# A decoder layer on one core: where TensorE's waits for banks, data and copied row maxima stand

## What is computed

```python
# x: (64, 128, 128), ctx: (64, 77, 128); 16 heads of 8 features
h = layernorm(x)
q, k = rope(h @ Wq.T + bq) * 8 ** -0.5, rope(h @ Wk.T + bk); v = h @ Wv.T + bv
x = x + softmax(causal(q @ k.T)) @ v @ Wo.T + bo                 # self attention
h = layernorm(x)
x = x + softmax(q2(h) @ k2(ctx).T * 8 ** -0.5) @ v2(ctx) @ Wo2 + bo2   # cross attention, 77 keys
h = layernorm(x)
top1, e = max(softmax(h @ router_w))                             # 8 experts, the eighth adds nothing
x = x + 2 * top1 * expert_e(h) + shared(h)                       # gated, 512 hidden
```

## Time and profile before

| what | value |
|---|---|
| time, median of 3 runs | 1080.29 (1079.55 to 1080.8) |
| profiled execution | 1076.56, span 1074.7, granted clock 0.995 |
| TensorE matmul busy | 987.1 (92%) |
| VectorE / ScalarE / GpSimd busy | 870.5 / 738.3 / 631.6 |
| masks L999, matmuls | x2048, 53.1 busy, 20.5 idle before, 14.8 of it for the DMA arena<-arena |
| DMAs arena<-arena (L391) | x512, 4.0 KB each |

### The profile page before, as it was taken

One profiled execution on the slowest core, in us unless ns is written; L12 is line 12 of the kernel. 1 busy time (PEld: TensorE's weight loads), 2 busy tenths in 40 slices (PEclk: granted clock), 3 DMA queues, 4 the chain that ended last, 5 costly groups with the idle time before them and its releaser, 6 DMA issues.

```text
span 1074.7 us, 45099 instructions
## 1 busy us (share of the span) xinstructions
PE 987.1 (92%) x16200; PEld 819.5 (76%) x16201; DVE 870.5 (81%) x2853; ACT 738.3 (69%) x1557; POOL 631.6 (59%) x1488
## 2 busy tenths in 40 slices
PE   1578999999999999999999999999999889999995
PEld 1356777777777777777777777777777889999995
DVE  3367999989999999989999999999996557777774
ACT  0266887888888787888878888887875245555552
POOL 0345667776767767676677767677664224444443
PEclk9999999999999999999999999999999999999998
DMA  5222111000010000000000000100010122222220
GB/s 132 70 71 71 33 29 32 28 28 27 25 32 26 30 25 28 29 25 30 25 29 28 25 30 25 31 26 30 26 28 24 60 66 71 72 68 71 67 67 5
DMA packets 66648, 44.27 MB, mean 41 GB/s; under 512 B 24135, under 2 KB 61451, under 8 KB 66592
## 3 DMA queue, kind: packets, MB, share of 16 engines
q1 hardware_dynamic: 55424, 30.35, 10.5%
q0 software_dynamic: 5312, 12.18, 3.3%
q10 hardware_dynamic: 5856, 0.99, 0.5%
HBM read 23.96 MB, written 18.29 MB: 39 GB/s over the span
## 4 chain that ended last, share of the span: by engine, by line
PE 62%; SPq 16%; DMA 6%; DVE 6%; issue 5%; ACT 2%; ACTq 1%; POOL 1%; DVEq 0%; POOLq 0%
SPq L391 12%; PE pv L1120 9%; PE scores L1300 6%; PE scores L1305 6%; PE ro L1316 6%; DMA arena<-arena 5%; PE scores L999 5%; PE ro L1175 4%; PE scores L1161 3%; PE ro L1137 3%; PE st L1230 3%; DVE arena L641 3%; PE scores L1167 2%; PE ro L1148 2%; PE pj L1143 2%
## 5 line engine op out<-in xcount | busy, mean ns | idle before, releaser
L641 DVE TENSOR_REDUCE arena<-scores 128x8 f16<-128x1024 f32 (+1 forms) x256 | 256.6, 1002 | 61.3 <-PE scores L1007 50.9
L919 ACT ACTIVATE arena<-scores 128x1024 f32<-128x1024 f32 (+1 forms) x256 | 262.6, 1026 | 57.7 <-PE scores L1016 44.6
L859 ACT ACTIVATE arena<-st 128x128 f16<-128x128 f16 (+2 forms) x256 | 155.0, 606 | 6.4 <-PE st L1230 5.4
L859 ACT ACTIVATE arena<-arena 128x512 f16<-128x512 f32 (+2 forms) x192 | 92.9, 484 | 71.4 <-POOL arena L453 51.4
L1120 PE MATMUL pv<-arena 128*32 128x128 f32 (+1 forms) x4096 | 139.1, 277 | 0.1
L1120 PEld LDWEIGHTS pv<-arena 128*32 128x32 f32 (+1 forms) x4096 | 104.6, 110 | 17.2 <-issue 10.1
L439 POOL TENSOR_TENSOR arena<-arena,neg_half 128x1 f32<-128x1 f32 x192 | 106.5, 555 | 15.0
L449 POOL TENSOR_TENSOR arena<-arena 128x256 f32<-128x256 f32 x64 | 46.5, 726 | 81.5 <-DVE arena L633 81.5
L526 POOL DMA_INDIRECT out_dram<-x_tile x70 | 69.9, 998 | 38.6 <-POOL carried L525 26.1
L477 POOL TENSOR_TENSOR arena<-arena 128x128 f32<-128x128 f32 x128 | 51.8, 404 | 60.2 <-DVE arena L651 60.2
L814 DVE SCALAR_TENSOR_TENSOR half_hid<-tanh_s,scores 128x512 f32<-128x512 f32 x70 | 48.1, 688 | 40.7 <-ACT tanh_s L964 40.6
(11 more groups left out here) (175 smaller groups left out, 2696.5 us busy)
## 6 DMA issues: line engine op xcount, KB each, us to landing
x_tile<-xs SPq DMA_DIRECT2D x70, 129.0 KB, 2.1
arena<-arena SPq DMA_DIRECT2D x512, 4.0 KB
arena<-in_x_dram SPq DMA_DIRECT2D x64, 64.0 KB, 1.8
out_dram<-pay SPq DMA_DIRECT2D x64, 64.0 KB, 1.6
arena<-in_ctx_dram SPq DMA_DIRECT2D x64, 38.5 KB
w_gate<-in_L_ffn_gate_w_dram SPq DMA_DIRECT2D x7, 256.0 KB, 2.6
w_up<-in_L_ffn_up_w_dram SPq DMA_DIRECT2D x7, 256.0 KB, 3.0
w_down<-in_L_ffn_down_w_dram SPq DMA_DIRECT2D x7, 256.0 KB, 4.1
```

What stands on the lines that cost most here:

```text
L641: v.tensor_reduce(nmax[:, n, :].rearrange("p (m r s) -> p r m s", r=2, s=SLOT)[:, u, :, 0:HG], pair(s)[:, :, 0:HG * keys].rearrange("p m ( ...
L859: return a.activation(to, of, ACT.Copy)
L919: a.activation(e32[0:rows, 2 * n + u, :], scores[0:rows, 1024 * s:1024 * (s + 1)], ACT.Exp).then_inc(sexp_done[n][u], 1)
```

## The change

The six pieces wait for the bank first and for the data second; `two_turns` waits for both banks, writes the masks, and only then waits for the operands of both computations. The waits are the same, no matmul, DMA or other engine's instruction is added or removed.

```diff
@@ two_turns
                 if has1:
-                    ready1(b1, p1)
                     turn(pe, b1, *after1)
                 if has2:
-                    ready2(b2, p2)
                     turn(pe, b2, *after2)
                 for h in range(4):
                     if has1 and mask1 is not None:
                         mask_round(s1, u1, mask1, h)
                     if has2 and mask2 is not None:
                         mask_round(s2, u2, mask2, h)
+                if has1:
+                    ready1(b1, p1)
+                if has2:
+                    ready2(b2, p2)
                 for g in range(HG):
@@ project_out, xT_of
             def project_out(b, p, n, *users):
+                turn(pe, b, *users)
                 wait(pe, oT_ready[n], b + 1)
-                turn(pe, b, *users)
...
             def xT_of(b, p, n, *users):
+                turn(pe, b, *users)
                 if n == 0:
                     wait(pe, x_in_s[p], 8 * b + 16 - 8 * p)
                 else:
                     wait(pe, (resid_done[0], xn3_ready)[n - 1], b + 1)
-                turn(pe, b, *users)
```

## The result

On the chip of the first profiles the changed kernel takes 1065.43 us (median of 4, 1063.24 to 1068.15), the kernel before 1079.92 (median of 4, 1078.38 to 1080.8): a ratio of 0.988, 95% interval 0.986 to 0.990, 14.5 us less. The forecast was 1071.0, with a range of 1067.5 to 1078.5.

A forecast was written before the change was run, and what follows sets the result against it. The loop was taken as close to TensorE-bound, with the copies' landing binding every second step. 0.28 a pair over 25 pairs (7.0) plus 1.8 and 0.5 from unrolled steps, 9.3 off 1080.3, gave 1071.0 us, range 1067.5 to 1078.5.

The forecast's parts named there:

- A: Loop step, every second one, whose first masks wait for the landing of SyncE's row-maxima copies; A to B took 11.95.
- B: The other loop step, whose masks follow the preceding matmul in TensorE's own order; B to A took 12.33.
- Masks, A and B: First self pair: masks no longer wait for copies or threshold registers; gain 0.19 in A, 0.09 in B.
- R: Moment of the first load of real rounds (L1007) behind the masks; the rest of the step hangs behind it.
- What this adds: One more wait instruction or register computation behind the masks, twice a step; bounds 0 to 0.11, taken as nothing.
- rival 1: Extra wait behind the masks partly bare, 0.05 a place, 0.15 of the 0.28 per pair lost; 1075.7 us, chance 0.17.
- rival 2: Splitting the masks-and-rounds group breaks load overlap, 0.15 lost at each place; slower, 1084.6 us, chance 0.08.
- Second cross pair: L1033's load behind hidden product L727: threshold registers now sit behind the bank's wait; cost 0 to 0.12, taken 0.06.
- rival 3: Last wait in the text sits on the load, so the cross pair gains 0.06 instead; 1069.5 us, chance 0.12.
- Second self pair: Load after the row maximum frees its bank: one of two queued instructions goes; gain 0.03 in A, none in B.
- xT 2: xT of the third normalisation, in B: the swap brings 0.05 at the load, of which 0.03 gets on.
- Rival 4: Another link (VectorE, or ScalarE between R and the copies) takes up the 0.22; 1078.5 to 1080 us, chance 0.09.

The follow-up runs named there:

- e7n: Changed kernel without the scatter, plus one more long-satisfied wait in each of two helpers behind the self-attention masks; 1068.50 us, ratio to the kernel before 0.9585.
- e3n: Changed kernel without the scatter, cross pairs' operand waits put back ahead of their bank waits; 1061.63 us, ratio to the kernel before 0.9525.
- e6n: Changed kernel without the scatter, SyncE's row-maxima copies ahead of its load of x and cross pairs' old wait order; 1057.63 us, ratio 0.9499.
- e2n: Kernel before without the scatter, with only the six one-wait swaps; 1074.75 us, ratio to the kernel before 0.9650.
- e5n: Changed kernel without the scatter, SyncE's copies of the row maxima issued ahead of its load of x; 1058.16 us, 4.4 less than an.
- bn: Kernel before with GpSimd's indirect scatter DMA replaced by a tiny vector operation; 1074.85 us, ratio to the kernel before 0.9632.
- an: Changed kernel with GpSimd's indirect scatter DMA replaced by a tiny vector operation; 1062.54 us, ratio to the kernel before 0.9511.
- e1n: Kernel before without the scatter, with only `two_turns` changed; 1062.73 us, ratio to the kernel before 0.9541.
- b0: Kernel before, unedited, measured and profiled again on another chip, scatter kept; 1114.49 us, ratio 1.0007.
- a0: Changed kernel, unedited, measured and profiled on the same chip as b0, scatter kept; 1108.07 us, ratio to the kernel before 0.9951.

## Why the forecast was right in kind and short in size

*What bounds the kernel.* Right. A was bound by the landing, B by TensorE's order, and both were met in after where the text said: masks ahead of the copies in A, rounds 0.36 behind them.

*Masks, A and B.* Right. R to R from B to A was forecast at 12.11 and took 12.11. That it is exact is luck in part: the 12.33 of the forecast is from masks to masks, R to R took 12.31, so 0.20 was gained and not 0.22.

*What this adds.* I took nothing, and in B the rounds follow the masks after 0.18 as before: rival 1 is out in this form. e7n shows that it was close: the next instruction in that place costs 0.05, what the rival took, and two cost 0.13. The Trainium skill ("Advanced Engine Details and Errata", Network/Comms) has 50 to 100 ns for a semaphore's reading from the sequencer; 0.05 for one added instruction and 0.13 for two agree with that, and the point of the case is that behind 0.19 of masks one such reading is free and a second isn't.

*The split group* (rival 2, slower). Out: the load behind the masks carries a wait or stands behind one and still starts 0.18 after the first mask, where the masks' matmuls take 0.40. This agrees with the Trainium skill, "TensorEngine Tiling (Array Packing)", Key Properties, which ties a drain to a change of mode.

*Second cross pair.* The direction and the loss of 0.06 were right on its own row: L727 ends at 507.04, the load starts 0.12 later, 0.06 more than in the earlier trace rows.

```profile
506.36 0.68 DVE L727 TENSOR_TENSOR hidT<-half_hid,scores 128x512 f32<-128x512 f32 x1
507.16 0.12 PEld L1033 LDWEIGHTS scores<-arena 28*77 28x77 f16 x2
```

So rival 3 is out. That it is just 0.06 was luck in part, as it was taken as the middle of 0 to 0.12. And as a term of the sum it was counted too high: putting the old order back (e3n) gave 0.03 in the even step and nothing in the odd one. In the odd one, which leads to A, the landing covers it (e6n brings it out), and part is made up at the wait behind.

*Second self pair and xT 2.* The masks of A's second pair start at 525.08, and their row names "issue" with 0.16 where the earlier trace rows had 0.19: the 0.03 of the forecast. The swap of xT 2 got 0.03 in the sum and is worth nothing by e2n, and *project_out* was counted at nothing, rightly. The six swaps together: e2n, nothing.

*Where the sum failed.* The path was right and two of its terms were too small. The first is A to B: forecast to lose 0.06, it lost 0.15 from R to R (11.96 to 11.81; 0.155 by the medians of the loop). The medians of each load, counted from R, show where. Rounds and values right behind R of A: 0.04, which the sum had at nothing; A's masks now end 0.17 ahead of their rounds, and the rows have 0.34 from R to the loads of the values (523.26 to 523.60) where before had 0.37. That this goes with the distance and with nothing else of the change is shown by e5n, where it is gone. Second self pair: 0.04 (forecast 0.03). Second cross pair: a loss of 0.04, as 0.02 of the 0.06 at its load is made up right behind it. B's masks: 0.10 (forecast 0.09). From these masks to R: 0.01, at nothing in the sum.

The second term is the written-out head: I had 2.3, and the traces show 3.2 on the first chip. bn and an differ there by 4.5 (172.1 against 167.6), but some 2 of it is probably the clock: between 80 and 90 us bn was granted 0.66 on average (part of it at the 1.2 GHz level) and its step there took 15.2, while the kernel before on the first chip was granted 1.00 and took 13.2; an and after were granted 0.83. I had counted one link in each of seven steps; e1n's row of the qkv matmul begins at 167.6 as an's does, so the gain is that of the turns, but by which link isn't shown.

Together, on the traces: forecast 7.0 + 2.3 = 9.3, measured 8.3 in 24 pairs, 0.3 in the steps behind them and 3.2 in the head, 11.8. The medians differ by 14.5, of which these 11.8 are seen in steps; without the scatter they differ by 12.3. The profiled execution of before (1076.56) was faster than all of its other runs, and that of after lost some 3 to the clock. What the remaining 2.7 of the medians are is open; with the 11.8 alone the result would have lain inside the range.

*Rival 4* (the copies aren't shortened in fact) is out on the first chip, by the 12.11. On the two chips where kernels with the scatter were profiled, something of its kind is true: another link, the stall behind the scatter, takes up most of the gain in the loop. I had looked for such a link on VectorE and ScalarE; the trace of before has only its small form, L641 of B 0.58 after R where bn has 0.50.

## What to carry to other kernels

A wait belongs behind whatever in its queue doesn't need it: here the sixteen mask matmuls gave 0.19 of cover, enough for one wait or register computation and not for two. Swapping two waits with nothing between them was worth nothing measurable, even where rows of the trace showed 0.05 between the forms: what followed waited for something else anyway. And before a small gain is taken or thrown away, measure on more than one chip: the same change was worth 1.2% on one and 0.5% on two others (counting its main part alone in one of them).

## What the runs showed of the hardware

GpSimd's indirect DMA (1.09 us on its engine, 129 KB) held TensorE's loads and its signals until about 1.3 us after its start on the two chips of the experiments where kernels with it were profiled: VectorE's row maximum started 1.42 to 1.50 after it in every step of the loop in b0 and a0. On the first chip the hold is short: the row maximum of B starts 0.64 to 0.73 after the DMA, which is 0.1 later, counted from R, than without it, and costs 0.07 a pair of steps. On a third chip of the experiments the kernel before fell from 1115 to 1075 us without the DMA, and a plain DMA of the same block from the same queue (0.64 us on the engine) cost nothing that the times show. Its mechanism stays open. In a kernel that has such a DMA in each step, on a chip that holds so long, work of TensorE that ends just ahead of it, or within 1.3 us behind it, is the wrong place to look for gains.
